# Moving work in the opening of a one-core projection, gather and feed-forward kernel: three gate products ahead of a scan, and the sums of marks behind the fourth tile

## The chip, the cores and the metric

The kernel runs on one core of a Trainium2 chip. The metric is the device time of one execution in microseconds (us). A core has TensorE (matmuls into eight banks of PSUM), VectorE, ScalarE, GpSimd (called POOL in the profile) and SyncE (SP), which here only issues DMAs. Each engine takes its instructions in program order and waits on semaphores.

## The reference, cut to what matters

```python
# x (16, 512, 512), ctx (16, 512, 1024), all float32
h = layernorm(x); h = rmsnorm(h, g_res) @ W_in.T + b_in
p = rmsnorm(ctx, g_init)[..., :512]                # one row for each patch
s = scan(lambda state, row: a * state + b * row, p) # a is about 0.001, b a constant
y = s[plug] + h                                     # plug: running count of marked places, from the mask
x = x + y
z = layernorm(x); prev = z shifted by one row
xr = mu_r * z + (1 - mu_r) * prev; xk = mu_k * z + (1 - mu_k) * prev
out = x + sigmoid(xr @ W_r.T) * (relu(xk @ W_k.T) ** 2 @ W_v.T)
```

## The kernel before

The 16 batches are called quarters here, numbered from Batch(0, 0); the first is Batch(0, 0), the second Batch(0, 1). Every quarter has 512 rows, in T = 4 tiles `t` of 128, and 512 columns, in C = 4 chunks `c`. Each float32 product is made of three matmuls (`product`, L561 to L563): high by high, high by low, low by high. ScalarE writes the high part (`xt_hi`, `xr_hi`, `wr_hi`, all L813) and VectorE the low part by a subtraction (L1003).

A quarter passes these steps:

- **Projection.** `project_tile(b, t, c)` multiplies the turned x by W_in, into banks 4 to 7 for the first quarter and 0 to 3 for the others.
- **Scan.** VectorE makes `u` from a context load (L1060). In the first two quarters the scan is one product of TensorE with a table of decays (`scan`, bank 3, and bank 7 for the second quarter), which needs `u_hi` and `u_lo`; VectorE adds the bias (`scan_out`, L1014) and SyncE or ScalarE stores `scanned` in `s_rows`. From the third quarter on the scan is four steps of VectorE (`scan_step`), each behind a shifting DMA into `above`.
- **Gather.** POOL adds rows of `s_rows` to the x in `ring` with four indirect DMAs (L505), one per tile; `dep_added[t]` counts their landing. `rows_added` waits for all four.
- **add_x** (L1170) adds the projection to `ring[t]`; only then is bank `t` free. Then follow the statistics, `norm_b`, 16 transposes on TensorE (`turn`), ScalarE's copies into `turned` (`turned_out`), and the mixes: ScalarE's `carry` (L862), VectorE's `mix_next` (L1136), ScalarE's high part, VectorE's `mix_low`. Mixes 0 to 3 give `xr`, 4 to 7 `xk`.
- **Products.** `gate_product` (`wr` by `xr`, banks 4 to 7), `key_product` (`wk` by `xk`, banks 0 to 3), relu and square on ScalarE (L909, L911), `ka_low` on VectorE, and `value_product` (`wv`).

The marks from which the gather's places are made are summed by `sum_marks` (nine small matmuls, L782 and L784) in the first quarter's projection; VectorE's `patches` turn them into indices.

The order of work is written out by hand for each engine. `iteration(b)` runs on every engine for b = -1, 0, 1 and on; in it `nxt` is b + 1 and `new` is b + 2. Iteration -1 has branches of its own (`is_first(nxt)`, `first_steps`), and so has iteration 0 (`is_first(b)`). The weights W_r, W_k, W_v are loaded by SyncE in the opening into buffers that are free then; W_r goes into `xt` once the first quarter's four gathers have landed and the second's `x_lo` is done. The second quarter's scan uses bank 7, and so the gate product of tile 3 waits for `scan_out`.

Of the kernel before, what the change touches and what calls it, by code (L numbers as in the profile page):

```python
# [89 lines left out]
def build(nc, x, x_turned, ctx, patch_lens, w_in, b_in, columns, g_init, w_r, w_k, w_v, out):  # L90
# [3 lines left out]
    C = D // P  # L94
    T = S // P
# [11 lines left out]
    with ExitStack() as stack:  # L107
# [203 lines left out]
        def _(sp):  # L311
# [90 lines left out]
                                     gate[:, T - 1, half_tile(h)]).then_inc(half_stored[h], 16)  # L402

            store_scan(Batch(0, 1))
            rows_added(sp, Batch(0, 1))
            reached(sp, far_over, Batch(0, 1), 1, 1)
            load_ctx(Batch(0, 2))

# [149 lines left out]
        def _(pe):  # L558
# [53 lines left out]
            def gate_product(b):  # L612


                order = [(t, c) for t in range(T) for c in range(C)]
                if is_first(b):
                    order = [(t, c) for c in range(C) for t in range(T)]
                for t, c in order:
                    if c == 0:
                        reached(pe, gated, b.plus(-1), T, t + 1)  # L620
                    if t == 0:
                        reached(pe, mix_lo_ready, b, 2 * C, c + 1 + (C if is_last(b) else 0))
                        if is_first(b):
                            pe.wait_ge(w_lo_ready[WR], c + 1)
                    if is_first(b) and c == 0 and t == T - 1:

                        reached(pe, s_copied, b.plus(1), 1, 1)
                    last = product(bank[4 + t][:, :], xr_hi[:, c, tile(t)], xr_lo[:, c, tile(t)],
                                   wt_hi[WR][:, c, :], wt_lo[WR][:, c, :], c == 0, c == C - 1)
                    if c == C - 1:  # L630
                        last.then_inc(r_done, 1)

            def first_key_product(b):


                for pair in ((0, 1), (2, 3)):
                    for c in range(C):
                        pe.wait_ge(w_lo_ready[WK], c + 1)
                        reached(pe, mix_lo_ready, b, 2 * C, C + c + 1)
                        for m in pair:  # L640
                            if c == 0:
                                reached(pe, x2_ready, b.plus(1), T, m + 1)
                            last = product(bank[m][:, :], wt_hi[WK][:, c, tile(m)], wt_lo[WK][:, c, tile(m)],
                                           xk_hi[:, c, :], xk_lo[:, c, :], c == 0, c == C - 1)
                            if c == C - 1:
                                last.then_inc(k_done, 1)

            def key_product(b):

# [82 lines left out]
            def first_steps(b):  # L732


                for c in range(C):
                    reached(pe, xt_lo_ready, b, 2, c // 2 + 1)
                    for t in range(T - 1):
                        project_tile(b, t, c)
                reached(pe, s_copied, b.plus(-1), 1, 1)
                reached(pe, far_over, b.plus(-1), 1, 1)  # L740

                reached(pe, x2_ready, b.plus(-1), T, T - 2)
                for c in range(C):
                    project_tile(b, T - 1, c)
                pe.wait_ge(ident_ready, 2)
                turn(b.plus(-1))

                reached(pe, yt_ready, b.plus(-1), T, T)
                scan(b)
                far(b)  # L750

            def sum_limbs():

# [41 lines left out]
            for c in range(C):  # L795
                reached(pe, xt_lo_ready, Batch(0, 0), 2, c // 2 + 1)
                pe.wait_ge(w_lo_ready[WIN], c + 1)
                for t in range(T):
                    project_tile(Batch(0, 0), t, c)
                    if c == 0 and t == 1:  # L800
                        sum_marks()
                    if c == 0 and t == 2:
                        pe.wait_ge(decay_lo_ready, 1)
                        scan(Batch(0, 0))
# [6 lines left out]
        def _(act):  # L811
# [53 lines left out]
            def mix_hi(b, first, last):  # L865

                for i in range(first, last):
# [4 lines left out]
                            act.wait_ge(zero_ready, 1)  # L872
                        carry(b, 0)
                    if is_first(b) and i == 0:

                        u_high(b.plus(1))
                    elif i + 1 < 2 * C:
                        carry(b, i + 1)
                    which, c = mix_row(b, i)
# [6 lines left out]
                        reached(act, v_done, b.plus(-1), T, T)  # L886
                    copy((xr_hi, xk_hi)[which][:, c, :], scratch[:, 2 + i % 2, :]).then_inc(mix_hi_ready, 1)
                    if is_first(b) and i == 0:
                        carry(b, 1)
                    if is_first(b) and i < C - 1:  # L890
                        weight_hi(WR, i + 1, i + 2)
# [32 lines left out]
            def iteration(b):  # L924
# [33 lines left out]
                if is_first(nxt):  # L958
# [1 line left out]

                    reached(act, far_over, nxt, 1, 1)
                    squares_c(new)
                    weight_hi(WR, 0, 1)
                    turned_out(nxt)
                if nxt.exists(B) and not is_last(nxt) and not is_first(nxt):
                    turned_out(nxt)
# [23 lines left out]
        def _(dve):  # L990
# [244 lines left out]
            def iteration(b):  # L1235
                nxt, new = b.plus(1), b.plus(2)
                if is_first(nxt):
                    x_lo(new, 1)
                    add_x(nxt, 0)
                    statistics_b(nxt, 0)  # L1240
                    add_x(nxt, 1)
                    statistics_b(nxt, 1)
                    statistics_a(new, 2)
# [8 lines left out]
                    norm_b(nxt, 0, T - 1)  # L1252
                    norm_b(nxt, T - 1, T)
                    scan_input(new)
                    weight_lo(WR, 0, 1)
                    stats_a(new, T)
                    mix_next(nxt, 0)
                    u_low(new)
                    mix_low(nxt, 0)
                    mix_next(nxt, 1)  # L1260
                    scan_out(new)
                    weight_lo(WR, 1, 2)
                    mix_low(nxt, 1)
                    mix_next(nxt, 2)
                    weight_lo(WR, 2, 3)
                    mix_low(nxt, 2)
# [251 lines left out]
```

## Time and profile before

| | |
|---|---|
| device time, median of 3 runs | 763.65 us (763.37 to 764.11) |
| profiled execution, its own time | 761.57 us |
| its span | 760.0 us |
| TensorE busy | 745.4 us, 98% |
| VectorE busy | 586.7 us, 77% |
| ScalarE busy | 405.5 us, 53% |
| POOL busy | 171.7 us, 23% |
| DMA, mean over the span | 132 GB/s |

The busy times are of the profiled execution. Matmuls overlap, so that the distance between two starts says more than a matmul's own duration. All times in rows count from the start of the span.

### The profile page before, as it was taken

Reading aid. Unit: us, or ns where it says so; the run is one execution under the profiler, and the core shown is the slowest. Engines: PE = TensorE matmul, PEld = TensorE weight load, DVE = VectorE, ACT = ScalarE, POOL = GpSimd, SP = SyncE. Lnnn points to the kernel's source line nnn. Section 1 sums busy time; section 2 is a strip of 40 time slices with the busy share of each in tenths; the row PEclk is TensorE's granted clock in tenths of the full one; section 3 lists DMA queues with packets and bytes.
Section 4 is the critical chain, followed back from the end, with each engine's and each line's share of the span. In section 5 each row is a group of like instructions: output and inputs, shape, how many; then the busy total and the mean of one; then the engine's idle time right before and its main releaser. Section 6 shows DMA issues by size and latency. Waiting matters only on the chain.

```text
span 760.0 us, 11067 instructions
## 1 busy us (share of the span) xinstructions
PE 745.4 (98%) x3432; PEld 616.0 (81%) x3433; DVE 586.7 (77%) x1063; ACT 405.5 (53%) x666; POOL 171.7 (23%) x163
## 2 busy tenths in 40 slices
PE   7988999999999999999999999999999999999998
PEld 5866788888888888888888888888888888888887
DVE  7888996887869778696876879778696977867462
ACT  4177354754545556453754545465364655544860
POOL 6441230313131031312113131121312113130000
PEclk9999999999999999999999999999999999999999
DMA  8667371726446272633716355281634627240011
GB/s 308 172 194 187 117 200 56 206 98 154 138 112 180 69 185 104 159 135 93 205 54 162 129 137 166 79 222 56 153 125 109 193 67 192 96 125 14 1 56 56
DMA packets 51453, 100.02 MB, mean 132 GB/s; under 512 B 5134, under 2 KB 5390, under 8 KB 51388
## 3 DMA queue, kind: packets, MB, share of 16 engines
q1 hardware_dynamic: 41900, 82.46, 31.6%
q0 software_dynamic: 9216, 16.78, 13.4%
q8 instruction: 14, 0.23, 0.1%
q14 instruction: 35, 0.29, 0.1%
q10 hardware_dynamic: 288, 0.27, 0.1%
HBM read 64.26 MB, written 21.76 MB: 113 GB/s over the span
## 4 chain that ended last, share of the span: by engine, by line
PE 92%; DMA 4%; POOL 1%; DVE 1%; issue 1%; ACT 0%; SPq 0%; DVEq 0%; POOLq 0%
PE bank L561 29%; PE bank L562 29%; PE bank L563 29%; PE bank L697 3%; POOL ring L505 1%; DMA ring<-s_rows,patch_now 1%; DMA xt<-in_L_ffn_W_r 1%; PE bank L791 1%; DMA ring<-s_rows,patch_of 1%; DMA above<-u 1%; DMA s_rows<-scanned 1%; PE bank L770 0%; DMA ctx_rows<-in_ctx 0%; DMA lens<-in_mask_BxS_if 0%; POOL rs_a L459 0%
## 5 line engine op out<-in xcount | busy, mean ns | idle before, releaser
L505 POOL DMA_INDIRECT ring<-s_rows,patch_now x60 | 99.9, 1665 | 228.8 <-DMA s_rows<-scanned 198.1
L1136 DVE SCALAR_TENSOR_TENSOR scratch<-turned,cols,scratch 128x512 f32<-128x512 f32 x128 | 94.4, 748 | 32.0 <-ACT scratch L862 21.9
L1003 DVE TENSOR_TENSOR xr_lo<-scratch,xr_hi 128x512 fp32r<-128x512 f32 x124 | 85.1, 688 | 39.8 <-ACT xr_hi L813 38.9
L813 ACT ACTIVATE turned<-bank 128x512 f32<-128x512 f32 x64 | 33.1, 604 | 131.1 <-PE bank L697 131.1
L561 PE MATMUL bank<-wi_hi,xt_hi 128*128 128x512 f32 x256 | 101.9, 398 | 0.0
L561 PE MATMUL bank<-xk_hi,wk_hi 128*128 128x512 f32 x256 | 100.0, 391 | 1.0 <-DVE xk_lo L1003 0.6
L563 PE MATMUL bank<-wi_hi,xt_lo 128*128 128x512 f32 x256 | 100.6, 393 | 0.0
L562 PE MATMUL bank<-wi_lo,xt_hi 128*128 128x512 f32 x256 | 100.5, 393 | 0.0
L561 PE MATMUL bank<-wr_hi,xr_hi 128*128 128x512 f32 x256 | 100.1, 391 | 0.0
L562 PE MATMUL bank<-wr_lo,xr_hi 128*128 128x512 f32 x256 | 100.0, 391 | 0.0
L563 PE MATMUL bank<-wr_hi,xr_lo 128*128 128x512 f32 x256 | 99.8, 390 | 0.0
L563 PE MATMUL bank<-xk_hi,wk_lo 128*128 128x512 f32 x256 | 99.6, 389 | 0.0
L562 PE MATMUL bank<-xk_lo,wk_hi 128*128 128x512 f32 x256 | 99.6, 389 | 0.0
L561 PE MATMUL bank<-wv_hi,xr_hi 128*128 128x512 f32 x240 | 94.4, 394 | 2.6 <-DVE xr_lo L1003 2.6
L562 PE MATMUL bank<-wv_lo,xr_hi 128*128 128x512 f32 x240 | 94.0, 392 | 0.0
L563 PE MATMUL bank<-wv_hi,xr_lo 128*128 128x512 f32 x240 | 93.9, 391 | 0.0
L862 ACT ACTIVATE scratch<-turned,cols 128x512 f32<-128x512 f32 x128 | 89.5, 710 | 0.5
L813 ACT ACTIVATE xr_hi<-scratch 128x512 fp32r<-128x512 f32 x124 | 77.9, 628 | 21.1 <-DVE scratch L1136 19.1
L1217 DVE TENSOR_TENSOR gate<-bank,gate 128x512 f32<-128x512 f32 x63 | 42.6, 689 | 54.2 <-PE bank L563 54.2
L898 ACT ACTIVATE gate<-bank 128x512 f32<-128x512 f32 x64 | 37.2, 593 | 68.9 <-PE bank L563 68.8
L813 ACT ACTIVATE xk_hi<-scratch 128x512 fp32r<-128x512 f32 x64 | 40.5, 632 | 45.5 <-DVE scratch L1136 44.8
L909 ACT ACTIVATE scratch<-bank 128x512 f32<-128x512 f32 x64 | 38.2, 597 | 41.1 <-PE bank L563 37.7
(148 smaller groups left out, 1267.1 us busy)
## 6 DMA issues: line engine op xcount, KB each, us to landing
ring<-in_x SPq DMA_DIRECT2D x16, 1024.0 KB, 5.2
out<-gate SPq DMA_DIRECT2D x63, 256.0 KB, 2.1
xt<-in_x_turned SPq DMA_DIRECT2D x14, 1024.0 KB, 7.2
above<-scanned SPq DMA_DIRECT2D x42, 224.0 KB, 2.7
ctx_rows<-in_ctx SPq DMA_DIRECT2D x15, 512.0 KB, 5.9
s_rows<-scanned SPq DMA_DIRECT2D x15, 256.0 KB, 2.5
above<-u SPq DMA_DIRECT2D x14, 224.0 KB, 2.7
gate<-in_L_xattn_W_in SPq DMA_DIRECT2D x4, 256.0 KB, 3.5
```

The source lines that it names most:

```text
L505: pool.indirect_dma_start(ring[b.slot][:, t, :], None, s_rows[:, :], bass.IndirectOffsetOnAxis(ap=rows, axis=0), compute_op=ALU.add).then_ ...
L561: nc.tensor.matmul(where, lhs_hi, rhs_hi, start=start, stop=False)
L562: nc.tensor.matmul(where, lhs_hi, rhs_lo, start=False, stop=False)
L563: return nc.tensor.matmul(where, lhs_lo, rhs_hi, start=False, stop=stop)
L697: last = nc.tensor.transpose(first_bank(b, t)[:, tile(c)], normed[:, t, c * P:(c + 1) * P], ident[:, :])
L813: return nc.scalar.activation(to, of, ACT.Copy)
L862: nc.scalar.activation(scratch[:, i % 2, :], turned[:, c, 0:S], ACT.Copy, scale=cols[:, 3 + which, c:c + 1]).then_inc(carried, 1)
L898: nc.scalar.activation(gate[:, t, :], bank[4 + t][:, :], ACT.Sigmoid).then_inc(gate_ready, 1)
L909: nc.scalar.activation(scratch[:, m % 2, :], bank[m][:, :], ACT.Relu).then_inc(relu_ready, 1)
L1003: return nc.vector.tensor_tensor(to, whole, high, ALU.subtract)
L1136: nc.vector.scalar_tensor_tensor(scratch[:, 2 + i % 2, :], turned[:, c, 1:S + 1], cols[:, 1 + which, c:c + 1], scratch[:, i % 2, :], ALU.m ...
L1217: nc.vector.tensor_tensor(gate[:, t, :], bank[4 + t][:, :], gate[:, t, :], ALU.mult).then_inc(gated, 1)
```

## The change

TensorE sums the marks behind the first quarter's fourth tile. In iteration 0 it makes three gate products before the second quarter's scan, which stood at the end of iteration -1, and goes through the gate product in another order; the key product takes the third and the fourth bank one after the other. ScalarE rounds the first chunk of W_r behind the first `carry`, not ahead of `turned_out`, and `u_high` goes behind the first `xr_hi`. VectorE's low parts are put in an order that fits. SyncE loads the third context after two gathers of the second quarter instead of four.

```diff
@@ SyncE, ahead of the iterations
             store_scan(Batch(0, 1))
-            rows_added(sp, Batch(0, 1))
+            for t in range(T // 2):
+                reached(sp, dep_added[t], Batch(0, 1), 16, 16)
             reached(sp, far_over, Batch(0, 1), 1, 1)
             load_ctx(Batch(0, 2))
@@ TensorE, gate_product
                 if is_first(b):
-                    order = [(t, c) for c in range(C) for t in range(T)]
+
+                    order = [(t, c) for c in range(2) for t in range(T - 1)] + [(T - 1, 0), (T - 1, 1)]
+                    order += [(t, c) for c in range(2, C) for t in range(T)]
                 for t, c in order:
+                    if is_first(b) and (t, c) == (0, 1):
+                        scan(b.plus(1))
+                        far(b.plus(1))
@@ TensorE, first_key_product
-                for pair in ((0, 1), (2, 3)):
-                    for c in range(C):
+                order = [(m, c) for c in range(C) for m in (0, 1)] + [(m, c) for m in (2, 3) for c in range(C)]
+                for m, c in order:
+                    if m == 0:
                         pe.wait_ge(w_lo_ready[WK], c + 1)
                         reached(pe, mix_lo_ready, b, 2 * C, C + c + 1)
...
@@ TensorE, first_steps
                 reached(pe, yt_ready, b.plus(-1), T, T)
-                scan(b)
-                far(b)
@@ TensorE, the first quarter's projection
                     project_tile(Batch(0, 0), t, c)
-                    if c == 0 and t == 1:
+                    if c == 0 and t == T - 1:
                         sum_marks()
@@ ScalarE, mix_hi
                     if is_first(b) and i == 0:
-
-                        u_high(b.plus(1))
+                        weight_hi(WR, 0, 1)
                     elif i + 1 < 2 * C:
                         carry(b, i + 1)
...
                     if is_first(b) and i == 0:
+                        u_high(b.plus(1))
                         carry(b, 1)
@@ ScalarE, iteration
                     squares_c(new)
-                    weight_hi(WR, 0, 1)
                     turned_out(nxt)
@@ VectorE, iteration -1
-                    x_lo(new, 1)
                     add_x(nxt, 0)
                     statistics_b(nxt, 0)
+                    x_lo(new, 1)
                     add_x(nxt, 1)
...
                     scan_input(new)
-                    weight_lo(WR, 0, 1)
                     stats_a(new, T)
                     mix_next(nxt, 0)
+                    weight_lo(WR, 0, 1)
+                    mix_low(nxt, 0)
                     u_low(new)
-                    mix_low(nxt, 0)
                     mix_next(nxt, 1)
-                    scan_out(new)
                     weight_lo(WR, 1, 2)
                     mix_low(nxt, 1)
+                    scan_out(new)
                     mix_next(nxt, 2)
```

The order of TensorE's instructions behind the sixteen transposes (L697) shows where the scan (`u_hi`, `u_lo`, by `decay`) stood, before:

```order
L697 MATMUL bank<-ident,normed 128x128 x3
L561 MATMUL bank<-u_hi,decay_hi 128x512 [waits u_lo_ready,yt_ready]
L562 MATMUL bank<-u_lo,decay_hi 128x512
L563 MATMUL bank<-u_hi,decay_lo 128x512
L300 TENSOR_LOAD far_table [waits table_ready]
```

And in the changed kernel, at the same place:

```order
L703 MATMUL bank<-ident,normed 128x128 x3
L562 MATMUL bank<-wr_hi,xr_hi 128x512 [waits wr_lo_ready,mix_lo_ready,yt_ready]
L563 MATMUL bank<-wr_lo,xr_hi 128x512
L564 MATMUL bank<-wr_hi,xr_lo 128x512
...
L562 MATMUL bank<-u_hi,decay_hi 128x512 [waits u_lo_ready]
L563 MATMUL bank<-u_lo,decay_hi 128x512
L564 MATMUL bank<-u_hi,decay_lo 128x512
L300 TENSOR_LOAD far_table [waits table_ready]
```

Three gate products of three matmuls each now stand ahead of the scan; two of the three are left out here. The first waits for the low parts of W_r and of the first mix, where the scan waited for `u_lo`.

VectorE's order from `scan_input` (the row with `u<-scratch`) on, before:

```order
L1060 SCALAR_TENSOR_TENSOR u<-scratch,rs_c,g_ctx 128x512 [waits u_lo_ready,rs_c_done]
L1003 TENSOR_TENSOR wr_lo<-xt,wr_hi 128x512 [waits wr_hi_ready]
...
L1136 SCALAR_TENSOR_TENSOR scratch<-turned,cols,scratch 128x512 [waits carried,yt_ready]
L1003 TENSOR_TENSOR u_lo<-u,u_hi 128x512 [waits u_hi_ready]
L1003 TENSOR_TENSOR xr_lo<-scratch,xr_hi 128x512 [waits mix_hi_ready]
L1136 SCALAR_TENSOR_TENSOR scratch<-turned,cols,scratch 128x512 [waits carried]
L1014 TENSOR_TENSOR scanned<-bank,bias 128x512 [waits s_stored,s_done]
```

In the changed kernel:

```order
L1063 SCALAR_TENSOR_TENSOR u<-scratch,rs_c,g_ctx 128x512 [waits u_lo_ready,rs_c_done]
...
L1139 SCALAR_TENSOR_TENSOR scratch<-turned,cols,scratch 128x512 [waits carried,yt_ready]
L1006 TENSOR_TENSOR wr_lo<-xt,wr_hi 128x512 [waits wr_hi_ready]
L1006 TENSOR_TENSOR xr_lo<-scratch,xr_hi 128x512 [waits mix_hi_ready]
L1006 TENSOR_TENSOR u_lo<-u,u_hi 128x512 [waits u_hi_ready]
L1139 SCALAR_TENSOR_TENSOR scratch<-turned,cols,scratch 128x512 [waits carried]
L1006 TENSOR_TENSOR wr_lo<-xt,wr_hi 128x512 [waits wr_hi_ready]
L1006 TENSOR_TENSOR xr_lo<-scratch,xr_hi 128x512 [waits mix_hi_ready]
L1017 TENSOR_TENSOR scanned<-bank,bias 128x512 [waits s_stored,s_done]
```

W_r's first low part moved behind the first mix, `u_lo` behind the first `xr_lo`, and `scan_out` (the last row) behind the second `wr_lo` and the second `xr_lo`.

## Rows read from the trace of the kernel before

**Rows 1.** The page, busy time of each engine: us, share of the span, instructions.
```profile
PE 745.4 (98%) x3432; PEld 616.0 (81%) x3433; DVE 586.7 (77%) x1063; ACT 405.5 (53%) x666; POOL 171.7 (23%) x163
```

**Rows 2.** The windows view, 90 us to the end; columns as in its head line.
```profile
core 0: us, PE busy (x) PEld busy (x) DVE busy (x) ACT busy (x) POOL busy (x), PEclk, DMA share, GB/s
90.00:760.00 670.00, 666.89 (x3069) 555.88 (x3067) 510.45 (x912) 360.77 (x590) 137.00 (x109) 1.00 0.43 123
```

**Rows 3.** Timeline of TensorE, first quarter: start us, us, what, [idle before].
```profile
15.65 0.63 PE L563 MATMUL bank<-wi_hi,xt_lo 128*128 128x512 f32 x1
...
18.34 0.66 PE L561 MATMUL bank<-u_hi,decay_hi 128*128 128x512 f32 x1
...
19.65 0.63 PE L561 MATMUL bank<-wi_hi,xt_hi 128*128 128x512 f32 x1
...
22.21 0.44 PE L561 MATMUL bank<-wi_hi,xt_hi 128*128 128x512 f32 x1
```

**Rows 4.** Timeline of VectorE, first quarter.
```profile
17.39 0.69 DVE L1003 TENSOR_TENSOR u_lo<-u,u_hi 128x512 fp32r<-128x512 f32 x1
...
26.20 0.43 DVE L1043 TENSOR_SCALAR v_a<-mv_a 128x4 f32<-128x4 f32 x1
```

**Rows 5.** Timeline of TensorE, from the transposes to the key product.
```profile
40.90 1.94 PE L697 MATMUL bank<-ident,normed 128*128 128x128 f32 x16
46.16 0.75 PE L561 MATMUL bank<-u_hi,decay_hi 128*128 128x512 f32 x1 [3.33 <-DVE u_lo L1003]
...
49.66 0.39 PE L563 MATMUL bank<-wr_hi,xr_lo 128*128 128x512 f32 x1
...
59.43 0.39 PE L561 MATMUL bank<-xk_hi,wk_hi 128*128 128x512 f32 x1
```

**Rows 6.** The chain that ended last, 35 to 67 us: start us, us, what.
```profile
35.88 5.33 DMA xt<-in_L_ffn_W_r
...
43.20 0.62 ACT turned L813
...
48.52 1.98 DMA s_rows<-scanned
...
57.59 5.58 DMA ring<-s_rows,patch_now
63.31 3.18 DMA ctx_rows<-in_ctx
```

**Rows 7.** Timeline of VectorE, 46 to 77 us.
```profile
46.11 0.69 DVE L1003 TENSOR_TENSOR xr_lo<-scratch,xr_hi 128x512 fp32r<-128x512 f32 x1
...
47.80 0.69 DVE L1014 TENSOR_TENSOR scanned<-bank,bias 128x512 f32<-128x512 f32 x1 [0.32 <-PE bank L563]
...
64.16 0.69 DVE L1003 TENSOR_TENSOR xk_lo<-scratch,xk_hi 128x512 fp32r<-128x512 f32 x1
...
69.43 0.75 DVE L1060 SCALAR_TENSOR_TENSOR u<-ctx_rows,rs_c,g_ctx 128x512 f32<-128x512 f32 x1
...
76.14 1.29 DVE L1003 TENSOR_TENSOR xr_lo<-scratch,xr_hi 128x512 fp32r<-128x512 f32 x2
```

**Rows 8.** Timeline of ScalarE, 66 to 69 us.
```profile
66.52 1.06 ACT L849 ACTIVATE ctx_squared<-ctx_rows 128x1024 bf16<-128x1024 f32 x1 [2.39 <-DMA ctx_rows<-in_ctx]
...
68.62 0.58 ACT L909 ACTIVATE scratch<-bank 128x512 f32<-128x512 f32 x1
```

**Rows 9.** DMA issues, in 64 to 71 us and of the whole: KB each, us to landing.
```profile
xt<-in_x_turned SPq DMA_DIRECT2D x1, 1024.0 KB, 10.2
...
above<-u SPq DMA_DIRECT2D x1, 224.0 KB, 5.2
...
above<-scanned SPq DMA_DIRECT2D x42, 224.0 KB, 2.7
```

**Rows 10.** Timeline of TensorE, 65 to 81 us.
```profile
65.00 0.47 PE L561 MATMUL bank<-xk_hi,wk_hi 128*128 128x512 f32 x1 [0.43 <-DVE xk_lo L1003]
...
76.88 0.79 PE L561 MATMUL bank<-wv_hi,xr_hi 128*128 128x512 f32 x1 [2.35 <-DVE xr_lo L1003]
...
80.39 0.39 PE L563 MATMUL bank<-wv_hi,xr_lo 128*128 128x512 f32 x1
```

More of the change, by code:

```diff
@@ L633, in first_key_product @@
             def first_key_product(b):
-                for pair in ((0, 1), (2, 3)):
-                    for c in range(C):
+                order = [(m, c) for c in range(C) for m in (0, 1)] + [(m, c) for m in (2, 3) for c in range(C)]
+                for m, c in order:
+                    if m == 0:
                         pe.wait_ge(w_lo_ready[WK], c + 1)
                         reached(pe, mix_lo_ready, b, 2 * C, C + c + 1)
[L640 to L646, printed above, removed]
+                    if c == 0:
+                        reached(pe, x2_ready, b.plus(1), T, m + 1)
+                    last = product(bank[m][:, :], wt_hi[WK][:, c, tile(m)], wt_lo[WK][:, c, tile(m)],
+                                   xk_hi[:, c, :], xk_lo[:, c, :], c == 0, c == C - 1)
+                    if c == C - 1:
+                        last.then_inc(k_done, 1)
             def key_product(b):
```

## The prediction

> **What bounds the kernel now.** I read the page first. TensorE is busy 745.4 us of 760.0, 98% of the span [rows 1]. A busy share of an average says little, so next come the windows. From 90 us on, TensorE is busy 666.89 of 670.00 us at the full granted clock [rows 2]. Behind the first quarters there is no wait to win or to lose. Whatever moves the moment at which TensorE is in step again, near 77 us, moves the end by as much, and nothing else in this change can. The chain that ended last goes the same way: matmuls to the end, and only before 77 us other engines and DMAs.
>
> So the opening has to be walked through. TensorE has three weak places there, seen in its timeline. First, the granted clock is low between 15.5 and 22.2 us: matmuls of 512 columns follow each other every 0.43 us (three from 18.34 to 19.65) instead of every 0.23 [rows 3]. Second, it is idle 3.33 us until 46.16, and its clock is then low until 49.6 [rows 5]. Third, it is idle 2.35 us until 76.88 and slow again until 80.4 [rows 10]. What TensorE waits for at 76.88 is VectorE's low part of a value operand, at 76.14, which stands in VectorE's order behind the first scan step of the third quarter, and that one behind the transfer into `above` [rows 7, 9].
>
> **The change, part by part.**
>
> *The marks.* The nine small matmuls went between the second and the third projected tile, from about 16.1 to 16.9. Without them the third tile runs from 16.1 to 17.4 (three times 0.43). The scan that follows needs `u_lo`, which ends at 17.39 + 0.69 = 18.08 [rows 4]. TensorE therefore stands still some 0.7 us which the marks had covered, and pays for the marks behind the fourth tile: the second column chunk starts near 21.5, not 20.93. That is 0.6 us at the low clock, and 0.3 us once the clock is back at 22.2, since half of what is left undone would have taken half the time. The projections have no other gap up to the transposes at 40.90 [rows 5], so the first quarter's transposes end 0.3 later: +0.3. If the pause cost its full length it would be +0.6; if `u_lo` came sooner, 0. VectorE's `patches` wait for the marks from 20.4 to 21.6, so `v_a` (26.20 + 0.43 = 26.63) [rows 4] and with it the root on POOL and the last two gathers come 1.0 later. The last gather landed near 35.7 and W_r's load was issued at 35.88 and took 5.33 [rows 6]; now it lands at 42.2. ScalarE's rounding of W_r no longer stands ahead of the four copies into `turned`, but behind the first `carry`, at about 44.7, so it has 2.5 us in hand. This costs nothing; the cover is those 2.5 us.
>
> *The reordered start.* `add_x(0)` goes ahead of `x_lo`: VectorE fills 1 us in which it waited. The normed tiles come earlier, but TensorE's own projections end at 40.9 + 0.3, so nothing is gained.
>
> *The scan behind three gate products.* TensorE resumed at 46.16 with the scan, and the first gate product followed at 47.6. Now the gate product is first. VectorE rounds W_r's low part behind the first mix, then writes `xr_lo`, which stood at 46.11 [rows 7]; with +0.3 from the front it starts at 46.3 and TensorE at 47.1, 0.9 later than it resumed. The three products are nine matmuls, 3.7 us at a clock that is low after such a gap [rows 5]. The scan begins at 50.8, takes 0.7 and is read 0.2 later: VectorE's `scan_out` goes from 47.80 to 51.7, which is +3.9. It now stands behind the second `xr_lo`, done at 49.7, so VectorE waits 2.0 there, and behind it wait `mix_next(2)`, the third and fourth low parts and ScalarE's `xr_hi` for them. The gate products themselves have enough operands: they end near 60.4 instead of 59.43.
>
> *What hangs on the scan.* Its store at 48.52 takes 1.98, the gathers begin 0.8 later, and the last of the four (57.59 + 5.58) lands at 63.17 [rows 6]. All move by 3.9: the last gather to 67.1, the second to 62.7, the first, by a landing some 5 us behind its start at 51.3, from 56.3 to 60.2. VectorE's way from `scan_out` to the last `xk_lo` was 64.16 - 47.80 = 16.4 us; 1.2 of it (one low part of W_r, one of `xr`) is already done, and 0.7 comes back in waits for the first gather and for ScalarE: 15.9. So the last `xk_lo` starts at 67.6, +3.4. TensorE, fed by it, ends the key products near 75.7.
>
> *The context load.* It waits for two gathers instead of four: 62.9 instead of 63.31, landing at 66.1. ScalarE had waited 2.39 us for it at 66.52 [rows 8]; now it arrives itself only at 67.4. So here 0.9 is lost instead of 3.4: the squares of the keys start at 69.8, not 68.62. Without this edit they would start 3 us later still. `u` (69.43 [rows 7]) stands behind two `wv_lo`, two `add_x`, two more `wv_lo`: 67.6 + 4.4 = 72.0.
>
> *The transfers.* The loads of the third quarter's x wait for the fourth gather: 67.2 instead of 64.2. In the trace `xt` landed 10.2 after its issue at 64.65, and the shifted `above` 5.2 after its issue, 0.55 behind `xt`, where it usually takes 2.7 [rows 9]: it queues behind the two 1 MB loads. 2.5 MB took 63.3 to 74.85, so 2 MB take 9.3: `xt` at 76.7, `above` at 77.3. VectorE comes free for the scan step at 77.4 by its own order. The third `ka_lo` then starts at 78.0 (was 76.14) and TensorE goes on at 78.9: +2.0 against 76.88.
>
> *The other reorderings* (key products three and four one after the other, where the last `k_done` doesn't move; x squares) are nothing: the same matmuls.
>
> **The sum, and its one open term.** By the walk TensorE is in step 2.0 us late. But its third gap is now 77.1 to 78.9, 1.8 us, where it was 2.35. After 2.35 the clock was granted low from 76.88 to 80.4, 3.5 us at half speed, worth 1.7 [rows 10]. If it doesn't fall after 1.8, the 2.0 become +0.3. The rows show a fall after 3.33 and 2.35, and none after the 0.43 at 65.0 [rows 10]; 1.8 is nearer the falls, but the runs will not all be alike. I take +1.2, between the two, and keep both ends. The skill's advice would give the lower end: the Trainium skill, TensorE: Matmul & The Clock Gate, "Why this matters for your kernels", warns only of idle gaps longer than either of these two. The trace does not agree with it, since the clock fell after 2.35 us.
>
> The profiled execution took 761.57 (span 760.0 and 1.57 around it), so it would give 762.8. The timed median is 763.65, 2.1 above; something in the opening or around it differs. I add the difference to the median: 764.8.
>
> **The rivals.**
> *Slower, the low clock of the first quarter lasts.* It stayed low 6.7 us from 15.5, although TensorE was busy but for the marks. Now there is a pause of 0.7 and the marks in it. If it stays low another stretch like the one from 46.16 (3.4 us), half is lost: +1.7, 766.5. It decides at the matmuls between 22 and 26 us: 0.43 or 0.23 apart. Against it: the same amount of work is done there.
> *Slower, the full price.* The clock falls in the 1.8 us gap in most runs: 765.65. Only that.
> *Faster, W_r's load was the brake.* In the trace it lands at 41.21, and the first `turned` copy follows once it is rounded; the last copy, at 43.20, had 0.3 to spare [rows 6]. Whatever W_r comes later than in this trace the old order pays, and the new one only beyond 2.5. In the timed runs, 2.1 us longer than the profiled one, it could be that. The new order would keep 2.2 of it: 764.8 - 2.2 = 762.6, and with the lower end of the sum 761.7. Against it: nothing shows the landing of another run.
> *It does nothing:* all of the late scan lies under the gap that was there. The walk speaks against it, since `above` and VectorE both come 1.9 later.
>
> **How the numbers follow.** About 0.2% (1.5 us) can be told from no change. Forecast, 764.0 to 765.1: 0.36. The full price 0.2, the lasting low clock 0.13, W_r 0.25, of which 0.15 is below 762.1, the rest 0.06. Range 762.0 to 766.6; the forecast's own is 764.0 to 765.1. Faster 0.2 (0.15 and most of the rest), same 0.46 (the forecast and the other 0.1 of W_r), slower 0.34.
>
> **What the profile would show.** TensorE's first `wr` matmul at 47.1 and the scan near 50.8; `scan_out` at 51.7 with a wait of 2 ahead of it; the last gather at 67.1; ScalarE no longer waiting for `ctx_rows`; the first `wv` matmul behind the gap at 78.9. The prediction is wrong if the clock is back before the three products (the scan then comes at 49.2 and 1.6 of the 3.9 vanish), if VectorE isn't what sets the key products, or if W_r came late in the timed runs.

## The result and the profile after

The changed kernel takes 767.56 us (median of 6 runs, 766.55 to 769.14), the kernel before 763.88 us beside it on the same chip (median of 6). One of the six runs before was a slow one of 1072.2 us, which the ratio leaves out. The ratio is 1.0065, with a 95% interval of 1.0046 to 1.0083. The kernel is slower: by 3.7 us by the medians above, by 3.9 if that run is left out, and by 5.0 (3.5 to 6.3) by the ratio. The forecast was 764.8 and the range ended at 766.6: the time lies outside it, 1.0 above.

| | before | after |
|---|---|---|
| profiled execution, its own time | 761.57 us | 767.76 us |
| its span | 760.0 us | 766.2 us |
| start of the first quarter's transposes | 40.90 | 42.73 |
| `scan_out` of the second quarter | 47.80 | 53.14 |
| TensorE restarts behind the last gap | 76.88 | 83.02 |
| from the transposes to that restart | 35.98 | 40.29 |

The page of the changed kernel answers to [rows 1]: TensorE and VectorE do the same work, in a longer span.

```profile
PE 747.0 (97%) x3432; PEld 616.7 (80%) x3433; DVE 587.3 (77%) x1063; ACT 405.6 (53%) x666; POOL 171.3 (22%) x163
```

The windows view of the changed kernel, 90 us to the end (start:end, length, busy time and count of each engine, granted clock, DMA share, GB/s), answers to [rows 2]:

```profile
90.00:766.00 676.00, 673.06 (x3104) 561.12 (x3102) 516.25 (x919) 361.96 (x592) 137.33 (x111) 1.00 0.43 123
```

Full clock, and a TensorE with next to no waits. So the loss must be in the opening, as the forecast had it. The timeline of TensorE there, changed kernel (start us, us, what, [idle before and its releaser]):

```profile
18.20 0.76 PE L562 MATMUL bank<-u_hi,decay_hi 128*128 128x512 f32 x1 [0.65 <-DVE u_lo L1006]
...
25.29 0.57 PE L564 MATMUL bank<-wi_hi,xt_lo 128*128 128x512 f32 x1
25.70 0.39 PE L562 MATMUL bank<-wi_hi,xt_hi 128*128 128x512 f32 x1
...
42.73 1.91 PE L703 MATMUL bank<-ident,normed 128*128 128x128 f32 x16
48.52 0.47 PE L562 MATMUL bank<-wr_hi,xr_hi 128*128 128x512 f32 x1 [3.89 <-DVE xr_lo L1006]
...
51.63 0.63 PE L562 MATMUL bank<-u_hi,decay_hi 128*128 128x512 f32 x1
...
83.02 0.50 PE L562 MATMUL bank<-wv_hi,xr_hi 128*128 128x512 f32 x1 [3.58 <-DVE xr_lo L1006]
```

Against [rows 3]: the pause of 0.65 us before the first scan is there, as forecast, and the matmuls keep the 0.43 us distance of the low clock (1.2 GHz) until 25.6, not until 22.2. That is about the 1.83 us by which the transposes start later. Against [rows 5]: TensorE resumes with a gate product behind a gap of 3.89 us and comes to the scan 3.11 us later. Against [rows 10]: the last gap is 3.58 us, not 2.35.

Two engines show what stood between. The timeline of VectorE, changed kernel:

```profile
53.14 0.69 DVE L1017 TENSOR_TENSOR scanned<-bank,bias 128x512 f32<-128x512 f32 x1 [1.93 <-PE bank L564]
...
69.31 0.69 DVE L1006 TENSOR_TENSOR xk_lo<-scratch,xk_hi 128x512 fp32r<-128x512 f32 x1
...
81.67 0.69 DVE L1084 SCALAR_TENSOR_TENSOR scanned<-above,u 128x512 f32<-128x512 f32 x1 [1.31 <-DMA above<-u]
```

The same scan step in the timeline of VectorE before, without a wait:

```profile
75.53 0.69 DVE L1081 SCALAR_TENSOR_TENSOR scanned<-above,u 128x512 f32<-128x512 f32 x1
```

The timeline of ScalarE, changed kernel:

```profile
71.44 1.06 ACT L853 ACTIVATE ctx_squared<-ctx_rows 128x1024 bf16<-128x1024 f32 x1 [2.16 <-DMA ctx_rows<-in_ctx]
```

`scan_out` waits 1.93 us, as forecast (2.0). The scan step, which found `above` there before, now waits 1.31 us for it. And ScalarE still waits 2.16 us for the third context, which [rows 8] had as 2.39 and which the change loads earlier. The chain that ended last, changed kernel (start us, us, what), says why:

```profile
64.26 7.15 DMA ctx_rows<-in_ctx
...
75.13 6.52 DMA above<-u
```

The context was issued at 64.26, once the second gather had landed, and took 7.15 us; in [rows 6] the same 512 KB took 3.18. The fourth gather suffered as well. The DMA issues of the changed kernel between 64.1 and 65 us (KB, us to landing; the gather is the fourth, issued at 62.99):

```profile
ring<-s_rows,patch_now POOLq DMA_INDIRECT x1, 8.6
```

It landed at 71.6, 8.6 us behind its start instead of 5.6 [rows 6]. SyncE issued the third quarter's x right then, at 71.78 (64.22 before), and `above` is queued behind it: 6.5 us, where [rows 9] have 5.2.

### The profile page after: what moved, and what is told of

Read it like the earlier page. It is cut to its first block, busy times and chain, and to the rows that moved or that the text cites. A ratio compares the mean times of both kernels' runs of the same rounds, so it can differ in the third digit from the quotient of the medians.

```text
span 766.2 us, 11061 instructions
## 1 busy us (share of the span) xinstructions
PE 747.0 (97%) x3432; PEld 616.7 (80%) x3433; DVE 587.3 (77%) x1063; ACT 405.6 (53%) x666; POOL 171.3 (22%) x163
## 3 DMA queue, kind: packets, MB, share of 16 engines
HBM read 64.26 MB, written 21.76 MB: 112 GB/s over the span
## 4 chain that ended last, share of the span: by engine, by line
PE 93%; DMA 3%; DVE 2%; issue 1%; ACT 1%; POOL 0%; DVEq 0%; POOLq 0%; SPq 0%
PE bank L562 30%; PE bank L564 30%; PE bank L563 30%; PE bank L703 3%; DMA ctx_rows<-in_ctx 1%; DMA above<-u 1%; PE bank L795 1%; DMA ring<-s_rows,patch_now 1%; DMA s_rows<-scanned 0%; ACT turned L817 0%; DMA lens<-in_mask_BxS_if 0%; DVE u L1449 0%; DVE gate L1395 0%; DVE xr_lo L1006 0%; DVE u L1063 0%
## 5 line engine op out<-in xcount | busy, mean ns | idle before, releaser
L562 PEld LDWEIGHTS bank<-xk_hi,wk_hi 128*128 128x128 f32 x256 | 48.0, 188 | 15.3 <-DVE ring L1173 2.7
```

What stands on the lines that cost most here:

```text
L562: nc.tensor.matmul(where, lhs_hi, rhs_hi, start=start, stop=False)
```

## The experiments

Each was timed beside the kernel before. Single executions of one kernel differ: the kernel before alone gave 759.1 to 766.9 us beside the experiments. So each run is read in two ways: by its ratio, and in one profile by the distance from the start of the first transposes to TensorE's restart behind the last gap. The second leaves out everything up to the transposes, and what comes behind the restart. It rests on one execution per kernel, so a few tenths of it mean nothing. And the stretch behind the restart isn't the same length in all: 681.5 to 684.9 us, mostly by the fall of the clock behind the gap and by late waits of TensorE for VectorE's low parts (1.3 us in e10). The table has all of the runs; where the trace gives no landing for the context, the last column has the gather alone.

| kernel | scan behind | context behind | median, us | ratio (95%) | transposes to restart | fourth gather, context: us to landing |
|---|---|---|---|---|---|---|
| before | 0 products | 4 gathers | 761.8 to 764.1 | 1 | 35.98 | 5.6, 3.2 |
| changed | 3 | 2 | 767.56 | 1.0065 (1.0046 to 1.0083) | 40.29 | 8.6, 7.2 |
| e1 marks only | 0 | 4 | 762.71 | 0.9988 (0.9971 to 1.0005) | 36.58 | 5.8, 3.4 |
| e2 all but marks | 3 | 2 | 768.26 | 1.0057 (1.0036 to 1.0077) | 40.35 | 8.2, 6.9 |
| e3 context after four | 3 | 4 | 766.74 | 1.0036 (1.0022 to 1.005) | 39.31 | 5.4, 3.2 |
| e4 filler | 3 | 2 | 767.43 | 1.0047 (1.0027 to 1.0066) | 40.33 | 7.9, 6.7 |
| e5 scan first | 0 | 2 | 763.73 | 1.0004 (0.9986 to 1.0022) | 36.43 | 8.1 |
| e6 scan first, context after four | 0 | 4 | 764.08 | 1.002 (1.0004 to 1.0036) | 36.18 | 5.4, 3.3 |
| e7 context only | 0 | 2 | 763.27 | 1.0000 (0.9981 to 1.0019) | 35.13 | 7.2, 6.0 |
| e8 scan behind one | 1 | 4 | 765.13 | 1.003 (1.0012 to 1.0048) | 36.85 | 5.5, 3.3 |
| e9 x order only | 0 | 4 | 763.41 | 0.9997 (0.9977 to 1.0018) | 35.33 | 5.1, 3.2 |
| e10 x order back | 3 | 2 | 766.73 | 1.0057 (1.0035 to 1.0079) | 38.95 | 7.2 |
| e11 marks and context | 0 | 2 | 762.55 | 0.9992 (0.9974 to 1.001) | 36.98 | 8.1 |
| e12 scan first, x order back | 0 | 4 | 762.1 | 0.9991 (0.9975 to 1.0008) | 35.77 | 5.4, 3.4 |
| e13 context at once | 3 | 0 | 765.26 | 1.005 (1.003 to 1.007) | 39.82 | 5.3, 4.8 |
| e14 scan first, context at once | 0 | 0 | 762.92 | 1.0007 (0.9987 to 1.0026) | 34.98 | 5.5 |
| e15 changed again | 3 | 2 | 768.23 | 1.0088 (1.0063 to 1.0113) | 40.33 | 8.4, 7.3 |

### First: the marks, the early context, the clock of the opening

**e1**, the kernel before with the marks behind the fourth tile:

```diff
-                    if c == 0 and t == 1:
+                    if c == 0 and t == T - 1:
                         sum_marks()
```

> The kernel before with the marks behind the fourth tile and nothing else. Theory 1 (the clock): TensorE then pauses 0.65 us ahead of the scan as in the changed kernel, the granted clock stays low to about 25.6 us instead of 22.2, and the transposes end 1.8 us later; everything behind them shifts by the same, so about +1.8 us on the end. Theory 2 (the late scan does nearly all, the opening's delay is swallowed by waits behind it): within 0.5 us of the kernel before.

0.9988: no cost that can be measured. The clock of the profiled execution was never low in the opening, although the pause was there (1.56 us at this clock), so the profile can't test the first theory; the time speaks against it. **e2**, the changed kernel with this line taken back:

> The changed kernel with the marks back behind the second tile. Theory 1: it wins back the 1.8 us of the opening and keeps the other four: about +4 us against the kernel before, scan_out near 51.5. Theory 2: the marks matter little, +5 to +6 us.

1.0057, and 40.35 us from the transposes to the restart. The loss is all there without the marks. **e3**, the changed kernel with the third context loaded as before:

```diff
-            for t in range(T // 2):
-                reached(sp, dep_added[t], Batch(0, 1), 16, 16)
+            rows_added(sp, Batch(0, 1))
             reached(sp, far_over, Batch(0, 1), 1, 1)
```

> The changed kernel, with the third context again loaded behind all four gathers. Theory 3 (the early load and the gathers hold each other up: the fourth gather landed 8.6 us behind its issue instead of 5.6, the context 7.2 instead of 3.2): the fourth gather lands near 68.6, the context near 71.8, the x loads start near 69.5 instead of 71.8, and the end is 1 to 2 us earlier than in the changed kernel. Rival (the early load helps or is neutral): the same or up to 1 us later.

Putting the context back does not cost 3 us, it gives about 1 back by the profile: the restart comes at 39.31, against 40.35 and 40.33 in the two runs beside it (e2, e4). By time it is 1.0036; that lies 2.2 us (0.4 to 4.0) below the changed kernel's 1.0065, but e2 and e4, timed beside it, are not clear of it. The context now takes 3.2 us again. The timeline of SyncE, e3:

```profile
66.64 0.35 SPq L322 DMA_DIRECT2D ctx_rows<-in_ctx  x1
67.31 0.38 SPq L316 DMA_DIRECT2D ring<-in_x  x1
```

Counted from the transposes (40.88 here, 42.73 in the changed kernel), the x goes out at 26.4 instead of 29.1, and the context lands at 29.0 instead of 28.7. The early load came only 0.3 us earlier to its end and held x back by 2.6 us.

**e4**, two matmuls that nobody reads, into a free bank, in the pause of the changed kernel (they add work, and leave nothing out):

```diff
                     if c == 0 and t == 2:
+                        for _ in range(2):
+                            nc.tensor.matmul(bank[7][:, :], xt_hi[:, 0, tile(0)], wt_hi[WIN][:, 0, :], start=True, stop=True)
                         pe.wait_ge(decay_lo_ready, 1)
```

> The changed kernel with two matmuls more, whose result nobody reads (they go into a bank that the next tile overwrites), in TensorE's pause ahead of the first scan. It costs 0.2 us of TensorE. Theory 1a (the pause alone keeps the clock low): the clock is back near 22.2 and the end 1.5 us earlier than in the changed kernel. Theory 1b (the sparse marks keep it low wherever they stand in that stretch): the clock is back at 25.6 again and the time is the same within 0.4 us.

1.0047: its interval holds the changed kernel's 1.0065, so nothing was won. The profile has 1.14 us of pause left and a clock that was never low in the opening, so it doesn't say whether the pause keeps the clock low. That marks and pause aren't the loss rests on e1 and e2.

### Second: the place of the scan

**e5** puts `scan` and `far` back ahead of the gate product, with ScalarE's and VectorE's order that belongs to it; all else is as changed:

```diff
@@ gate_product
-                    if is_first(b) and (t, c) == (0, 1):
-                        scan(b.plus(1))
-                        far(b.plus(1))
@@ first_steps
                 reached(pe, yt_ready, b.plus(-1), T, T)
+                scan(b)
+                far(b)
@@ ScalarE, mix_hi
+                        u_high(b.plus(1))
                         weight_hi(WR, 0, 1)
...
-                        u_high(b.plus(1))
                         carry(b, 1)
@@ VectorE
                     mix_next(nxt, 0)
+                    u_low(new)
                     weight_lo(WR, 0, 1)
                     mix_low(nxt, 0)
-                    u_low(new)
                     mix_next(nxt, 1)
+                    scan_out(new)
                     weight_lo(WR, 1, 2)
                     mix_low(nxt, 1)
-                    scan_out(new)
```

> The changed kernel with the scan (and what it needs: u_high, u_low, scan_out) again ahead of the gate products; the marks, the order of the products, ScalarE's W_r rounding behind the first carry and the context load behind two gathers stay as changed. Theory A (the late scan and the early context load are the whole loss): scan_out near 47.6 us of the span, and the end within 1 us of the kernel before, with up to 1 us left for the context load that meets the gathers. Rival B (the other reorderings cost too): 2 us or more above the kernel before.

1.0004: the whole loss is gone; the changed kernel lies 4.7 us (2.7 to 6.6) above it. In TensorE's timeline of e5 the restart comes 36.43 us behind the transposes:

```profile
43.68 1.91 PE L700 MATMUL bank<-ident,normed 128*128 128x128 f32 x16
80.11 0.79 PE L562 MATMUL bank<-wv_hi,xr_hi 128*128 128x512 f32 x1 [3.65 <-DVE xr_lo L1005]
```

**e6** is e5 with e3's edit:

> As the run with the scan first, and the context load again behind all four gathers, so that the marks, the orders of products and the W_r rounding are what is left of the change. Theory A: the kernel before within 0.7 us, or up to 1 us faster since VectorE and ScalarE have waits filled. Rival B: the left parts cost 1.5 us or more.

**e7** is the kernel before with the context behind two gathers, e3's edit turned round:

> The kernel before with the context load behind two gathers and nothing else. Theory 3 (the load and the last two gathers delay each other): the load is issued near 59.5 and takes 6 to 7 us instead of 3.2, the last gather lands 2 to 3 us later than 63.2, the x loads and the shifted rows come 2 us later, and the end is 1 to 2 us later. Rival: the context lands 1 us or more earlier, the squares start earlier and the end is the same or up to 1 us earlier.

1.0020 for e6: the late context gives nothing here either. 1.0000 for e7, where 1 to 2 us more were expected. Alone the early load disturbs the gathers too (7.2 us for the fourth), but ScalarE's wait for it falls from 2.4 to 0.5 us; gain and loss seem to cancel. **e8** has the scan behind one product instead of three (`(1, 0)` for `(0, 1)` in the condition), `scan_out` ahead of the second low part of W_r, and the context behind four gathers:

> The changed kernel with the scan behind one gate product instead of three, scan_out back behind the second mix, and the context load behind four gathers. If each product ahead of the scan costs its own time (1.3 us each at the low clock), scan_out comes 2.6 us sooner than with three, near 49 us, and of the 2.6 us that the kernel with the context behind four gathers lost against the kernel before, 1.5 to 2 are won back: about +0.5 to +1 us. Rival (the place of the first gate product is what costs, since TensorE starts later whatever follows): +2 us or more.

1.003, with the restart at 36.85. From e8 to e3 two more products go ahead of the scan: `scan_out` comes 2.6 us later behind the transposes (7.78 and 10.42) and the restart 2.5. Two products at the low clock are six times 0.43 us, 2.6. So by the profiles each costs about its own time, since everything up to the restart hangs on the scan. (e8 paid 0.9 for its one product against the kernel before, 0.7 against e6; one profile each.)

The times don't show this price. By its ratio e8 is 2.3 us (0.9 to 3.7) above the kernel before, more than the 0.5 to 1 expected and in reach of the rival's 2. In e6, e8 and e3, which have the context behind four gathers and differ in the place of the scan and what goes with it, the ratios are 1.002, 1.003 and 1.0036: e3 is only 0.5 us (-1.3 to 2.2) above e8 and 1.2 (-0.4 to 2.8) above e6, where the restarts are 2.5 and 3.1 apart. So the place of the scan is shown as the cause with the context behind two gathers, by e5; what each product costs is a reading of single profiles.

### Third: the order of x, and combinations

**e9** is the kernel before with `add_x(nxt, 0)` and its statistics ahead of `x_lo`:

> The kernel before with one edit: in VectorE's iteration -1 the first add_x goes ahead of x_lo. Theory C (x_lo now waits for the first gather, and the second quarter's projection waits for x_lo): VectorE waits 1 to 2 us for the gather, TensorE 0.5 to 2.5 us at its third column chunk in those executions in which the clock was full, and the end is 1 to 2 us later. Rival (as predicted, it fills a wait): the same within 0.5 us.

**e10** is the changed kernel with that taken back:

> The changed kernel with x_lo ahead of the first add_x again. Theory C: 1 to 2 us less than the changed kernel, so about +3 us against the kernel before, which is the late scan (+3.1 by the stretch from transposes to transposes) and the early context load behind it (+1). Rival: no difference to the changed kernel, +4 to +5.

**e11** is the kernel before with e1's and e7's edits:

> The kernel before with two parts of the change: the marks behind the fourth tile and the context load behind two gathers. Alone they gave 0.9988 and 1.0000 of the kernel before; the stretch from transposes to transposes was 0.8 us shorter with the early load. If both hold, 0.5 to 1.5 us below the kernel before; if what they gave was the draw of the executions, the same within 0.7 us.

**e12** is e6 with e10's edit:

> The changed kernel with the scan ahead of the gate products, the context load behind four gathers and x_lo ahead of the first add_x: left are the marks, the orders of the gate and key products and the W_r rounding behind the first carry. Theory A with C: the kernel with the scan first and the context behind four (+1.5 us) loses 1.5 to 2 us, so it is the kernel before or up to 1 us faster. Rival (the orders or the W_r rounding cost): +1 us or more.

e9 and e11 are no different from the kernel before, e10 not from the changed one. The order of x isn't free in the trace. With `add_x` ahead TensorE waits for `xt_lo` in the third chunk, from 0.4 us (e3) and 0.6 (e9) to 2.6 (e6), but not in the two profiles of the changed kernel, where the low clock lasts until 25.6 and 25.9. With `x_lo` ahead it never does, whether the clock was low (before, e7) or full (e1, e10, e11, e12, e14). The first transposes start at 42.4 us in the mean of the ten profiles with `add_x` ahead and at 41.0 in the mean of the seven others. The distance to the restart leaves this out, so it could be another part of the loss. The times don't settle it: e9 says no effect, e10 is 0.6 us (-1.6 to 2.8) below the changed kernel, and e6 is 2.2 us (0.5 to 4.0) above e12. This stays open.

### Fourth: was it the context beside the gathers?

**e13** is the changed kernel without the wait for gathers, so that the context goes out at 57.29, ahead of most of them:

```diff
-            for t in range(T // 2):
-                reached(sp, dep_added[t], Batch(0, 1), 16, 16)
             reached(sp, far_over, Batch(0, 1), 1, 1)
```

> The changed kernel with the third context loaded as soon as its buffer is free, behind no gather of the second quarter. Theory D (shared DMA engines are why the early load gives nothing): the load is issued near 58, before the gathers' rows move, takes under 5 us, the fourth gather lands 5.5 us behind its issue again and the x loads start 3 us sooner than in the changed kernel; TensorE restarts some 37.7 us behind the start of the first transposes (40 in the changed kernel), and the end is 2 us earlier than with the changed kernel. Rival (something else holds the squares or the restart): as the changed kernel, within 0.7 us.

**e14** does the same to e12:

> The kernel with the scan ahead of the gate products and x_lo ahead of the first add_x (0.9991 of the kernel before with the load behind four gathers), with the context loaded as soon as its buffer is free. Theory D: the squares of the keys are no longer held by the load, TensorE restarts 1 to 2 us sooner (34 to 35 us behind the start of the transposes instead of 36), about -2 us against the kernel before. Rival: VectorE holds the restart all the same, 0 to -1 us.

**e15** is the changed kernel once more, beside these two:

> The changed kernel once more, for its time on the same chip as the two others: +3.5 to +5 us against the kernel before, restart 40 us behind the start of the transposes.

The DMA issues of e13, first around the context and the first two gathers, then around the fourth gather:

```profile
ctx_rows<-in_ctx SPq DMA_DIRECT2D x1, 512.0 KB, 4.8
...
ring<-s_rows,patch_now POOLq DMA_INDIRECT x1, 5.3
```

The context takes 4.8 us instead of 7.2, the fourth gather 5.3 instead of 8.6, ScalarE doesn't wait for the context any more, and the scan step doesn't wait for `above`. In time, e13 is 3.0 us below e15, the changed kernel timed beside it (765.26 and 768.23), and e15 itself is 6.4 us above the kernel before there (1.0088), more than the 3.5 to 5 expected. But only a part of the 3.0 is that cause. The restart came only 0.5 us sooner, at 39.82, not at the expected 37.7; and in this execution the clock stayed full behind the last gap of 2.17 us. TensorE, e13:

```profile
80.41 0.50 PE L560 MATMUL bank<-wv_hi,xr_hi 128*128 128x512 f32 x1 [2.17 <-DVE xr_lo L1004]
80.75 0.39 PE L561 MATMUL bank<-wv_lo,xr_hi 128*128 128x512 f32 x1
80.98 0.40 PE L562 MATMUL bank<-wv_hi,xr_lo 128*128 128x512 f32 x1
```

What held the restart there is VectorE's own order, without a gap in it from the last `xk_lo` on but one of 0.46 us (for POOL's `rs_c`) and one of 0.16. VectorE, e13:

```profile
68.53 0.69 DVE L1004 TENSOR_TENSOR xk_lo<-scratch,xk_hi 128x512 fp32r<-128x512 f32 x1
...
73.47 0.75 DVE L1061 SCALAR_TENSOR_TENSOR u<-ctx_rows,rs_c,g_ctx 128x512 f32<-128x512 f32 x1 [0.46 <-POOL rs_c L477]
...
79.06 0.69 DVE L1082 SCALAR_TENSOR_TENSOR scanned<-above,u 128x512 f32<-128x512 f32 x1
```

In e14 the restart comes at 34.98, 0.8 us sooner than in e12, as expected, but the time doesn't fall: 1.0007, where 2 us less were expected. So with the scan first, sparing the kernel a late context wins nothing that can be measured.

No version beats the kernel before by more than can be measured: e12, e1 and e11 have the lowest ratios, and all their intervals hold 1.

## Why the prediction was wrong

The forecast put the change 1.15 us above the median of before, and 2.0 above it at the full price; 3.7 were measured by the medians, 5.0 by the ratio. Point by point:

- **Where it would be decided** was right. From 90 us on the work is the same, and the restart moved the end: 6.14 us later in the profile, and the execution 6.19 longer. That the two agree so well is partly luck, since the stretch behind the restart differs by up to 3.4 us between profiles (1.3 between the two of the changed kernel).
- **The marks and the pause** were right in the row (0.65 us for 0.7), and cost nothing that can be measured (e1, e2). The rise in the profiled execution at the transposes, 1.83 us, is the rival "the low clock of the first quarter lasts" by its signs (0.43 us apart until 25.6, priced 1.7). Nothing shows the change as its cause: the clock was low until 25.9 in e15, but until about 24.2 in e7, with the marks in their old place, until 22.3 in e9, until about 18 in e2, e5, e8 and e13, and in e1, e3, e4, e6, e10, e11, e12 and e14 not at all. It differs between kernels whose instructions up to there are the same: before and e7; changed, e3 and e13.
- **The scan behind three products** was right to a few tenths: `scan_out` 10.41 us behind the transposes, forecast 51.7 - 41.2 = 10.5, and 6.90 before. VectorE's way on was right too: the last `xk_lo` at 69.31 - 42.73 = 26.6, forecast 67.6 - 41.2 = 26.4.
- **The step that failed is "The context load"**, with "The transfers" that hang on it: "It waits for two gathers instead of four: 62.9 instead of 63.31, landing at 66.1", and the last gather at 67.1. It was issued as forecast (21.5 us behind the transposes, forecast 21.7), but I gave it the 3.18 us of [rows 6], where it had run after the last gather. Issued between gathers it takes 7.2 (e15: 7.3), and makes the fourth gather take 8.6 (e15: 8.4) instead of 5.6. So the squares of the context start at 28.7 behind the transposes, not 26.2; x goes out at 29.1, not 26.0; `above` is 1.3 us late for the scan step. The restart came 40.3 behind the transposes, not 37.7. e3 and e13, in which the two transfers take 3.2 to 5.4 us, show that it is the load's place among the gathers that makes them slow.
- **"Without this edit they would start 3 us later still"** fell with it. Without it those squares start at 29.0 (e3) instead of 28.7, and the kernel is a little faster. I had taken the edit to save nearly 3 of the scan's 3.4 us; it saves nothing, and the late scan is paid in full: +3.3 us by the profile (e3), and another 0.7 or so by the load (40.05, the mean of the five profiles with both, against 39.31). The five run from 38.95 (e10) to 40.35, so the 0.7 is no firm number.
- **A step that I misread and that did no harm**: the loads of x waited in the trace before not for the gather (63.17) but for VectorE's last `wk_lo`, which ends at 64.1 and whose weights lie in their buffer; they went out at 64.22. In e13 it is so again (68.43 and 68.59). In the changed kernel it is the gather, at 71.6.
- **A second term was too small: VectorE's own way.** In e13, where no transfer is late, VectorE needs 10.5 us from the last `xk_lo` to the scan step, and the forecast had 9.8. The restart at 39.8, for the forecast 37.7, is this 0.7, 0.8 by which `scan_out` came later in that execution (the clock granted from 44 to 56 us was 0.72 there, 0.86 in the changed kernel), 0.7 more up to `xk_lo`, and 0.15 less behind the step. For the changed kernel this means: with its own `xk_lo` at 26.6 and VectorE's 10.5 and 1.35 us from there, the restart would stand at 38.5 even without late transfers, and by e13 less its late `scan_out` at 39.0. So of the miss of 2.6 us in the restart 1.3 to 1.8 are the load's place and the rest is VectorE's order. The split is worked out, not measured apart.
- **The last gap** was 3.58 us instead of 1.8, and the clock fell behind it: 0.61 was granted from 84 to 88 us. Since it fell in the kernel before as well, the open term adds nothing, and the middle value that I took for it was 0.8 too low. How open it was is shown by the other runs: the clock fell behind gaps of 2.17 us (e14), 2.31 (e1, e8, e9), 2.32 (e3), 2.35 (before), 2.42 (e7) and 2.75 (e6), and not behind 2.17 (e13), 2.31 (e12) and 2.62 (e10). The Trainium skill, TensorE: Matmul & The Clock Gate, "Why this matters for your kernels", warns only of longer gaps; eight of these eleven disagree with it.
- **The reordered start** was put at "nothing is gained", without a look at `x_lo`, which it moves back. Its wait shows in the profiles of several experiments, though not in those of the changed kernel; what it costs is open (third part above).
- **The other rivals.** That W_r's load was the brake found nothing for it: e5, e6 and e12 keep its rounding behind the first `carry`, and are no faster than before. That the late scan is hidden was wrong, by e5.

By the profiles 3.3 for the late scan and 0.7 for the load are 4.1 with the rounding, between the 3.7 of the medians and the 5.0 of the ratio. The sum is shown better than its parts: by the ratios the late scan with the context behind four gathers costs 1.2 us (e3 over e6), and with the context behind two 4.7 (the changed kernel over e5), with wide intervals. It may be that the two edits cost more together than each alone; that is not shown.

## What to carry to other kernels

A short instruction that starts a long chain (scan, store, gather, load, next operand) should not be put behind work that only keeps an engine busy, even where the engine has an idle stretch before it: by the profiles the three products ahead of the scan were paid at about their length, and putting the scan back first took the whole loss away. A load that is issued earlier is not priced by the time that it took alone: look at what is in flight at its new place, both ways, since it also delays what stands there, and what waits for that. And where single executions of one kernel lie 1% apart, distances between two points of a profile suggest causes which the ratio can't tell apart; but they rest on one execution and say nothing of what lies outside the two points.

## What the runs showed of the hardware

- A plain load of 512 KB issued between four indirect gathers that add took 7.2 us instead of 3.2, and the last gather 8.6 instead of 5.6 (6.0 and 7.2 in e7). The Trainium skill, DMA: Bandwidth & Descriptors, "Issuing engines are not separate DMA queues", says that DMAs started by different engines run on the same sixteen DMA engines and interleave. The rows agree with it, since both transfers are slower side by side, and add the price. Issued ahead of most of the gathers (e13) the load took 4.8 and left the fourth gather at 5.3. Why the order makes this difference was not tried.
- The granted clock isn't the same in all executions of the same instructions. In the opening it was low (1.2 GHz) until 22.2 us before and until 24.2 in e7, which has the same instructions up to there; until 25.6 in the changed kernel, until about 18 in e13 and never in e3. Behind last gaps of 2.17 us each it fell in e14 and not in e13. The fall lasted 3.4 us in most profiles, which costs 1.7, and some 6 us in e5 (80.1 to 86.2), which costs 3. Over the whole of the kernel before the mean granted clock ran from 0.988 to 0.998. This can be a part of why that kernel took 759.1 to 766.9 us; how large a part was not worked out.
